# A recommender kernel on one core: twenty sparse gathers fetched row by row on SyncE instead of ten, and three rounds of the last layers placed inside the last tile

## What is computed

```python
mask = seq_inputs[:, :, 0] != 0
other_info = concatenate([dense_inputs] + [emb_sparse[i][sparse_inputs[:, i]] for i in range(3)])
seq_embed  = concatenate([emb_seq[i][seq_inputs[:, :, i]] for i in range(2)])      # 2048 x 40 x 128
item_embed = concatenate([emb_seq[i][item_inputs[:, i]] for i in range(2)])        # 2048 x 128
info = concatenate([q, seq_embed, q - seq_embed, q * seq_embed])                   # q: item_embed, repeated
h = sigmoid(info @ att_W1 + att_b1)            # 512 -> 80
h = sigmoid(h @ att_W2 + att_b2)               # 80 -> 40
att = softmax(where(mask, h @ att_Wf + att_bf, NEG_INF))
user_info = einsum('bl,bld->bd', att, seq_embed)
x = bn(concatenate([user_info, item_embed, other_info]))
x = prelu(x @ ffn_W1 + ffn_b1, ffn_a1)         # 456 -> 80
x = prelu(x @ ffn_W2 + ffn_b2, ffn_a2)         # 80 -> 40
return sigmoid(x @ out_W + out_b)              # 2048 x 1
```

## Time and profile before

| what | value |
|---|---|
| median of 3 runs | 1611.01 us (1609.24 to 1612.11) |
| the profiled execution's own time | 1607.81 us |
| its span, first to last instruction | 1606.0 us |
| PE busy | 1407.4 us, 88% of the span |
| POOL busy | 1198.4 us, 75% |
| DVE busy | 849.7 us, 53% |
| ACT busy | 398.4 us, 25% |
| granted TensorE clock, mean | 0.972 of full |

### The profile page before, as it was taken

How to read it: one execution, slowest core, us unless ns; L and a number is a source line. 1 busy time by engine, 2 the same in 40 slices (tenths; PEclk the granted TensorE clock), 3 DMA queues, 4 the chain that set the end, 5 groups by cost and what they waited for, 6 DMA issues and landing times.

```text
span 1606.0 us, 25922 instructions
## 1 busy us (share of the span) xinstructions
PE 1407.4 (88%) x7602; PEld 776.3 (48%) x7602; DVE 849.7 (53%) x2102; ACT 398.4 (25%) x725; POOL 1198.4 (75%) x1259
## 2 busy tenths in 40 slices
PE   0599999998989988898988888998889998989878
PEld 0355555554545444454544455545455554545432
DVE  5744647463554646365464634646464464636453
ACT  3422213221222212121131222212222221212123
POOL 7877777777777777777777777777777777777773
PEclk9999999999999999999999999999999999999975
DMA  8411121211111121111111112121111112111121
GB/s 165 105 28 47 27 47 28 47 28 27 48 27 48 28 46 29 27 47 28 48 28 47 28 27 48 28 47 28 46 29 27 48 28 46 28 27 28 28 27 14
DMA packets 61501, 63.51 MB, mean 40 GB/s; under 512 B 35845, under 2 KB 36179, under 8 KB 61359
## 3 DMA queue, kind: packets, MB, share of 16 engines
q0 software_dynamic: 40128, 41.17, 12.6%
q1 hardware_dynamic: 19170, 12.53, 3.1%
q10 hardware_dynamic: 2062, 8.08, 1.8%
HBM read 61.57 MB, written 0.11 MB: 38 GB/s over the span
## 4 chain that ended last, share of the span: by engine, by line
POOL 72%; issue 24%; PE 3%; DVE 1%; ACT 1%; POOLq 0%; DMA 0%; DVEq 0%
POOL hist L346 70%; POOL items L346 2%; DVE sums L892 1%; PE pre L530 0%; PE pre L542 0%; PE pre L531 0%; ACT pool L632 0%; PE turned L523 0%; PE pre L442 0%; PE mid L458 0%; PE turned L524 0%; PE pre L444 0%; PE mid L451 0%; DMA hist<-in_L_rec_emb_seq_dram,idx 0%; PE sums L399 0%
## 5 line engine op out<-in xcount | busy, mean ns | idle before, releaser
L346 POOL DMA_INDIRECT hist<-in_L_rec_emb_seq_dram,idx x1184 | 1131.4, 956 | 361.0 <-issue 361.0
L412 PE MATMUL grown<-pool,split 128*128 128x384 bf16 x4704 | 849.6, 330 | 39.7 <-DVE pool L795 39.6
L412 PEld LDWEIGHTS grown<-pool,split 128*128 128x128 bf16 x4704 | 454.5, 99 | 443.9 <-issue 155.5
L795 DVE TENSOR_SCALAR pool<-rel 128x768 bf16<-128x768 bf16 x784 | 382.2, 541 | 0.0
L919 DVE TENSOR_TENSOR prod_t<-turned,item_t 128x512 f32<-128x512 f32 x160 | 109.7, 688 | 401.0 <-ACT hist_t L657 400.8
L662 ACT ACTIVATE hidden<-pre 80x512 f32<-80x512 f32 x160 | 94.9, 593 | 612.7 <-DVE pre L927 601.3
L927 DVE TENSOR_TENSOR pre<-pre,item_part 80x512 f32<-80x512 f32 x160 | 111.0, 694 | 167.5 <-PE pre L444 167.5
L425 PE MATMUL turned<-ident,hist 128*128 128x128 f32 x592 | 99.1, 288 | 86.4 <-DMA hist<-in_L_rec_emb_seq_dram,idx 85.7
L442 PE MATMUL pre<-hist_t,w_hist 128*80 128x512 f32 x320 | 164.4, 595 | 0.0
L444 PE MATMUL pre<-prod_t,w_raw 128*80 128x512 f32 x320 | 163.4, 592 | 0.0
L892 DVE SCALAR_TENSOR_TENSOR sums<-hist,weight,sums 128x128 f32<-128x128 f32 x608 | 159.8, 348 | 0.0
(11 more groups left out here) (110 smaller groups left out, 466.8 us busy)
## 6 DMA issues: line engine op xcount, KB each, us to landing
sparse_rows<-in_L_rec_emb_sparse_dram SPq DMA_DIRECT2D x1280, 0.2 KB
hist<-in_L_rec_emb_seq_dram,idx POOLq DMA_INDIRECT x1184, 2.4
keys<-key_rows SPq DMA_DIRECT2D x28, 384.0 KB
hist<-in_L_rec_emb_seq_dram ACTq DMA_DIRECT2D x6, 672.0 KB
keys<-key_rows ACTq DMA_DIRECT2D x4, 384.0 KB
hist<-in_L_rec_emb_seq_dram ACTq DMA_DIRECT2D x2, 728.0 KB
sparse_rows<-in_L_rec_emb_sparse_dram,idx_sparse POOLq DMA_INDIRECT x38, 3.3
raw<-in_r_seq_inputs_dram SPq DMA_DIRECT2D x1, 600.0 KB, 8.4
```

The costliest lines, as they stand in the source:

```text
L346: gp.indirect_dma_start(rows, None, table, bass.IndirectOffsetOnAxis(ap=index, axis=0)).then_inc(landed, 16)
L412: last = nc.tensor.matmul(grown[n][:, 0:MC], split[n][:, c, k, :], hot[:, slot, n * MC:(n + 1) * MC], start=(c == 0 and k == 0), stop=(c = ...
L795: last = nc.vector.tensor_scalar(hot[:, slot, :], rel[half][:, :, 0:RC], float(c), None, ALU.is_equal)
```

## The change

Three constants change. `FETCHED` goes from 10 to 20, `SOONER = 3` is new, and `USER_AT` goes from 2 to 4, since the round in which the last tile's user vector is taken has another number.

SP now takes the twenty gathers in blocks of up to six, the six of one pair, lane by lane: 128 lanes for gathers 0 to 5, then 128 for 6 to 11, 128 for 12 to 17, and 128 for 18 and 19. These 512 lane visits are cut into 16 stages of 32. POOL makes 28 sparse gathers instead of 38.

The rounds of pairs 0, 1 and 2 move into the last tile, at g = 7 and ahead of that group's transposes, on PE, ACT and DVE. They use the PSUM banks `grown` and `sums` instead of `turned`, `pre1` and `mid`; DVE does `pick` ahead of `product` there. Five rounds stay at the end.

```diff
-    USER_AT = 2
-    FETCHED = 10
-    LANES = P // TILES
+    USER_AT = 4
+    FETCHED = 20
+    SOONER = 3
...
-            taken = [sp.alloc_register(f"row_number{i}") for i in range(FETCHED)]
+            taken = [sp.alloc_register(f"row_number{i}") for i in range(2 * NS)]
             halves = sparse_table.rearrange("v (h e) -> v h e", h=2)
-
-            def fetch_rows(first, end):
-                for lane in range(first, end):
-                    sp.load(taken, idx_sparse[lane:lane + 1, :, :].rearrange("p t n -> p (t n)")[:, 0:FETCHED])
-                    for i in range(FETCHED):
+            lanes = [(first, lane) for first in range(0, FETCHED, 2 * NS) for lane in range(P)]
+
+            def fetch_rows(stage):
+                for first, lane in lanes[stage * len(lanes) // TILES:(stage + 1) * len(lanes) // TILES]:
+                    count = min(2 * NS, FETCHED - first)
+                    numbers = idx_sparse[lane:lane + 1, :, :].rearrange("p t n -> p (t n)")
+                    sp.load(taken[0:count], numbers[:, first:first + count])
+                    for i in range(count):
                         row = sp.snap(taken[i], min_val=0, max_val=NS * V - 1)
-                        tile, n = i // NS, i % NS
+                        tile, n = (first + i) // NS, i % NS
                         sp.dma_start(sparse_rows[lane:lane + 1, tile, n * E:(n + 1) * E].rearrange("p (h e) -> p h e", h=2),
                                      halves[bass.ds(row, 1), :, :]).then_inc(sparse_fetched[tile // 2], 16)
 
             sp.wait_ge(sparse_idx_ready, 1)
-            fetch_rows(0, LANES)
+            fetch_rows(0)
             for tile in range(TILES - 1):
                 sp.wait_ge(picked_ready, tile + 1)
                 if tile + 2 < TILES:
                     load_keys(tile % 2, tile + 2)
-                fetch_rows((tile + 1) * LANES, (tile + 2) * LANES)
+                fetch_rows(tile + 1)
...
+            def sooner_rounds():
+                pe.wait_ge(part_ready, TILES - 1)
+                pe.wait_ge(picked_ready, TILES)
+                for p in range(SOONER):
+                    turn_sparse(p)
+                    if p > 0:
+                        ffn2(p - 1)
+                    ffn1(p)
+                    if p > 0:
+                        output(p - 1)
+                ffn2(SOONER - 1)
+                output(SOONER - 1)
...
+                    if last and g == SHARE:
+                        sooner_rounds()
                     if g < LAST:
                         turn_group(g + 1)
...
             pe.wait_ge(softmax_step, TILES * 2)
-            for p in range(PAIRS):
+            for p in range(SOONER, PAIRS):
                 turn_sparse(p)
-                if p > 0:
+                if p > SOONER:
                     ffn2(p - 1)
```

More of the change, by code:

```diff
@@ L203, in build @@
         items_landed = [sem(f"items_landed{h}") for h in range(2)]
-        sparse_fetched = [sem(f"sparse_fetched{p}") for p in range(2)]
+        sparse_fetched = [sem(f"sparse_fetched{p}") for p in range(-(-FETCHED // (2 * NS)))]
         sparse_landed = [sem(f"sparse_landed{p}") for p in range(PAIRS)]
@@ L513, in _ @@
                 body(TILES - 2 + half, half, PAIRS - 1, False, half == 1)
[L515 to L539, removed]
-                if p > 0:
-                    pe.wait_ge(score_ready, p)
-                nc.tensor.matmul(pre1[1][0:1, 0:W], ow[:, :], y2[:, :], start=True, stop=True).then_inc(score_done, 1)
             pe.wait_ge(softmax_step, TILES * 2)
-            for p in range(PAIRS):
+            for p in range(SOONER, PAIRS):
                 turn_sparse(p)
-                if p > 0:
+                if p > SOONER:
                     ffn2(p - 1)
                 ffn1(p)
-                if p > 0:
+                if p > SOONER:
                     output(p - 1)
@@ L649, in weigh, with copy_sparse, add_bias2, score_of @@
                 act.preload_act_table(ACT.Sigmoid)
+            def copy_sparse(p):
+                act.wait_ge(sparse_turned, p + 1)
+                k = SPARSE_B[1]
+                normalised(x_sparse[:, 0, :], 3, grown[0][:, 0:W])
+                normalised(x_sparse[0:k, 1, :], 4, grown[0][0:k, W:2 * W]).then_inc(sparse_copied, 1)
+            def add_bias2(p):
+                act.wait_ge(ffn2_done, p + 1)
+                nc.scalar.activation(z2[:, :], (sums if p < SOONER else mid)[0:H2, 0:W], ACT.Identity, bias=fb2[:, :]).then_inc(z2_ready, 1)
+            def score_of(p):
+                act.wait_ge(score_done, p + 1)
+                nc.scalar.activation(score[:, p * W:(p + 1) * W], sums[0:1, W:2 * W] if p < SOONER else pre1[1][0:1, 0:W], ACT.Sigmoid, bias=ob[:, :])\
+                    .then_inc(score_ready, 1)
+            def sooner_rounds():
+                for p in range(SOONER):
+                    copy_sparse(p)
+                    if p > 0:
+                        add_bias2(p - 1)
+                        score_of(p - 1)
+                add_bias2(SOONER - 1)
+                score_of(SOONER - 1)
             def body(tile, half, pair, first, last):
@@ L910, in add_rows, with prelu1, prelu2, sooner_rounds @@
                     user_row(tile)
+            def prelu1(p):
+                dve.wait_ge(ffn1_done, p + 1)
+                dve.wait_ge(part_ready, 2 * p + 2)
+                nc.vector.tensor_tensor(z1[:, :], grown[1][0:H1, 0:W], part[:, p * W:(p + 1) * W], ALU.add).then_inc(z1_step, 1)
+                dve.wait_ge(z1_step, 2 * p + 1)
+                nc.vector.tensor_scalar(n1[:, :], z1[:, :], 0.0, fa1[:, :], ALU.min, ALU.mult).then_inc(z1_step, 1)
+                dve.wait_ge(z1_step, 2 * p + 2)
+                nc.vector.scalar_tensor_tensor(y1[:, :], z1[:, :], 0.0, n1[:, :], ALU.max, ALU.add).then_inc(y1_ready, 1)
+            def prelu2(p):
+                dve.wait_ge(z2_ready, p + 1)
+                nc.vector.tensor_scalar(n2[:, :], z2[:, :], 0.0, fa2[:, :], ALU.min, ALU.mult).then_inc(n2_ready, 1)
+                dve.wait_ge(n2_ready, p + 1)
+                nc.vector.scalar_tensor_tensor(y2[:, :], z2[:, :], 0.0, n2[:, :], ALU.max, ALU.add).then_inc(y2_ready, 1)
+            def sooner_rounds():
+                for p in range(SOONER):
+                    if p > 0:
+                        prelu2(p - 1)
+                    prelu1(p)
+                prelu2(SOONER - 1)
             def body(tile, half, pair, first, last):
@@ L954, in body @@
                         ends = [first_hot + 3, first_hot + 5]
+                    if last and g == SHARE:
+                        pick()
+                        sooner_rounds()
                     if g < LAST:
                         product(g + 1, (g + 1) % 2)
-                    if g == SHARE:
+                    if g == SHARE and not last:
                         pick()
-                        if not last:
-                            dve.wait_ge(rel_ready, tile + 2)
+                        dve.wait_ge(rel_ready, tile + 2)
                     heat(to, other, first_hot, ends[0])
@@ L987, in _ @@
                 body(TILES - 2 + half, half, PAIRS - 1, False, half == 1)
[L988 to L1001, removed]
             for step in range(len(ROWS_AT)):
@@ L1005, in _ @@
                 if step > 0:
-                    prelu2(step - 1)
-                prelu1(step)
-            for p in range(len(ROWS_AT), PAIRS):
+                    prelu2(SOONER + step - 1)
+                prelu1(SOONER + step)
+            for p in range(SOONER + len(ROWS_AT), PAIRS):
                 prelu2(p - 1)
```

29 lines of the change are left out of this document (added).

## The result

| | before | changed |
|---|---|---|
| median | 1611.46 us (1609.24 to 1612.11, 4 runs) | 1924.43 us (1923.04 to 1925.70, 4 runs) |
| ratio | | 1.1945, 95% interval 1.1924 to 1.1966 |
| profiled span | 1606.0 us | 1923.9 us |
| mean granted TensorE clock | 0.972 | 0.873 |

The change makes the kernel 19.4% slower, 313 us. The range given was 1755 to 1965 us, the forecast 1861.

A forecast was written before the change was run, and what follows sets the result against it. POOL's gathers bound the kernel before; SP's row fetches, with key loads behind them, would after. 1496.3 us to tile 12's `relate` plus 359.9 gave a 1856 span; 1.8 and 3.2 on top gave 1861 us, range 1755 to 1965.

The forecast's parts named there:

- Where it bites: SP's key loads go out late behind row fetches; ACT first stalls 18 us, then every tile waits 30 us.
- The step of an issue and the stage: On SP, 0.42 us an issue, 3.63 us a lane, 115 us a stage of 32 lanes; a tile has 94.9.
- the load's price: SP's register load of six numbers: 0.98 us, the middle between 0.73 (in proportion) and 1.22 (all fixed).
- the sum: Total span of the changed kernel: 1496.3 us to `relate` in tile 12 plus 359.9 to the end, 1856.
- From the last stage to the end: From `relate` in tile 12: 260.1 + 25.8 + 1.2 + 16 + 17.8 + 38.95 = 359.9 us.
- The moved rounds alone: Rounds moved into the last tile, without SP's effect: -15.9 us in the tail, +17.2 in the tile, +3 by the clock.
- the fixed price: SP's load of six costs as much as one of ten, 1.22 us: period 124.9, time 1955 us; chance 31%.
- POOL's ten gathers: The ten sparse gathers POOL no longer makes, 12.5 us of POOL, bring nothing, as the tail's rounds hide them.
- SP keeps pace: Rival: SP's stage stays under 94.9 us, hurts no tile, only the end changes: 1615 us; chance 4%.
- SP's queue backs up: Rival: with 192 issues in a row a step grows from 0.42 to 0.5 us, adding 184 us: 2045; chance 3%.

The follow-up runs named there:

- Experiment 5: Changed kernel with 18 gathers by SP in twelve stages of 32 visits and the key loads issued by ACT, not SP: 1616.81 us.
- experiment 3: Kernel of experiment 1 with the pairs' row numbers 17 words apart, beginning at word 1, so at bytes 4, 8 and 12 of 32: 2068.97 us.
- experiment 7: Kernel of experiment 6 with all eight rounds of the last layers in the tail, as before the change: 1609.56 us, ratio 1.0001.
- experiment 6: Changed kernel with each lane visited once, one load of twenty numbers, eight lanes a stage, moved rounds kept: 1616.59 us, ratio 1.0040.
- experiment 1: Changed kernel with each pair's row numbers in a 32-byte piece of their own: 1855.17 us, ratio 1.1508.

## Why the prediction was right, point by point

- **Where it bites.** Right. The key load stands behind the row fetches, `relate` waits for keys in tiles 1 to 12 and not after, and the first wait is 17.5 us (18 forecast). Those of tiles 2 to 4 and 9 to 12 are 25.3 to 29.1 us (30 forecast), and those of tiles 5 to 8, behind the dear stages, 42.5 to 46.6. Experiment 5 shows the cause: take the keys out of SP's queue, and the loss is gone but for the rounds' part, with SP as late as ever.
- **The step of an issue and the stage.** Right for eight of the twelve long stages: 114.2 us (115), a period of 116.3 (117.0), a load of six at 0.99 us (0.98); the last six issues of stage 0 take 2.34 us (2.41).
- **The term that was mis-sized** is the load's price, "I take the middle, 0.98", with bounds of 0.73 and 1.22: in four stages it was 1.56 us, above the dearer bound. Those periods were 134.2 us for 117.0, 69 us in all; the other seven, at 116.3, gave 5 back. That nearly makes up the 68 us by which the span (1923.9) passed the sum (1856). I had looked for the price only in the number of registers, and the row that I had was of loads that all begin at the tile's first byte. That 1924 still lies inside 1755 to 1965 is in part luck: only one of three pairs lay badly. With all three so (experiment 3) the same mechanism took 2069.
- **From the last stage to the end**: 365.7 us from `relate` in tile 12 (1558.19) against 359.9. The way from tile 12's `relate` to `pick` took 290.2 for 285.9: its steps were 87.8 and 88.2 us and not 86.7, and the last stretch 114.1 for 112.5. The rounds took 18.2 (16), groups 7 to 9 17.2 (17.8), and the tail 38.97 (38.95).
- **The moved rounds alone** were forecast at some 4 us of loss (1609.6 of span for 1606.0), and are 7.0. They were placed where nothing covers them: `pick` is waited for (1.2 us), they take 18.2 us in the tile for 15.9 in the tail, and the lower granted clock costs groups 7 to 9 another 2.4. That is 5.9 us; the rest is open (experiment 7).
- **A slip in the sums**: a load of six at 1.2 us gives 1947 us by the prediction's own steps, not "1957"; the fixed price of 1.22 gives 1955. The forecast uses neither.
- **POOL's ten gathers** bring nothing, as said (experiment 7).
- **The rivals.** "SP keeps pace" became true once the loads were made fewer (experiment 6), and its time for that case, 1615 us, was met by 1616.6. "SP's queue backs up" is out: the 2560 issues of the changed kernel took 224, 225 and 306 ns (least, median, most), as the 1280 before, and experiment 5 has 2304 of them on end.

The Trainium skill (DMA: Bandwidth & Descriptors, "Latency and other measured facts") has the floor of a register load at about 600 ns. The trace agrees: loads of two take 0.74 us. Its rate of about 200 ns for each register (Runtime: NRT & Kernel Launch, "Instruction fetch mechanics") isn't found here: twenty would take 4 us by an estimate from it, and took 1.49. Under "Terms" that page of the Trainium skill has them as loads from HBM, and those here are from SBUF, so the two needn't contradict each other.

## What to carry to other kernels

An engine that looks idle has a budget, and it is the length of the loop that it serves. Count what stands in its queue ahead of the one transfer that others wait for; here a period of 123 us on average (1350.7 us over eleven) stood where 95 fitted, and a gain of nothing was bought with 313 us. A transfer that others wait for doesn't belong behind a long row of small ones: on ACT's queue it cost nothing here. And work moved out of a tail is best laid into the gaps of other work: here that gained 5 us, while in a block of its own it took its own waits along and lost 7.

## What the runs showed that I had not expected

A register load on SP from SBUF costs by its count and by its first byte. Beginning at a multiple of 16 bytes: 0.99 us for six numbers, 1.22 for ten, 1.49 for twenty. Not at such a multiple: 1.56 for six, with first bytes 4, 8, 12 and 24 of 32 alike. Two numbers are spared: they began at 8 of 16 in the change and took 0.74 in the median, and at a multiple of 16 in experiments 1 and 3, where stage 12 reads:

```profile
L324 SPq TENSOR_LOAD <-idx_sparse x32: 674/747/888, 1482.9 to 1534.4; - x32
...
L324 SPq TENSOR_LOAD <-idx_sparse x32: 672/747/822, 1701.1 to 1752.5; - x32
```

Loads of three to five, or of over six at other first bytes, weren't tried. Why it is so stays open. The way around it is free: fewer, longer loads, and numbers that begin at multiples of 16 bytes.
